# ScalarE's load of the table for Gelu and its copy of the last turned rows of the MLP change places

## What is computed

```python
attn_out = attn_out @ out_w + out_b + residual
out = rmsnorm(attn_out, postnorm_w)
out = jax.nn.gelu(out @ mlp_w1 + mlp_b1) @ mlp_w2 + mlp_b2
return out + residual
```

## Time and profile before

| what | value |
|---|---|
| median of 3 runs | 1889.08 us (1888.2 to 1889.91) |
| the profiled execution | 1890.01 us, of which the span is 1888.0 us |
| TensorE busy | 1640.7 us, 87% |
| VectorE busy | 1215.1 us, 64% |
| ScalarE busy | 894.8 us, 47% |
| GpSimd busy | 780.4 us, 41% |
| mean granted clock of TensorE | 0.94 |

### The profile page before, as it was taken

One profiled execution on the slowest core, in us unless ns is written; L12 is line 12 of the kernel. 1 busy time (PEld: TensorE's weight loads), 2 busy tenths in 40 slices (PEclk: granted clock), 3 DMA queues, 4 the chain that ended last, 5 costly groups with the idle time before them and its releaser, 6 DMA issues.

```text
span 1888.0 us, 34749 instructions
## 1 busy us (share of the span) xinstructions
PE 1640.7 (87%) x13615; PEld 1023.1 (54%) x13615; DVE 1215.1 (64%) x2153; ACT 894.8 (47%) x1855; POOL 780.4 (41%) x871
## 2 busy tenths in 40 slices
PE   5898998899997898888988989889998889889735
PEld 3675555565564655655555655646456465555303
DVE  4742478655886468855687457864588646983483
ACT  4454554545544445545454456444555544554202
POOL 5631249404573147702485034840457214770000
PEclk9998898999999999999988999999999999999857
DMA  6001014200331005100141101410042100510060
GB/s 186 1 2 36 1 21 55 42 23 1 44 43 35 19 1 69 25 28 19 18 55 22 44 4 24 62 36 19 1 53 36 33 19 1 69 25 1 13 91 11
DMA packets 73567, 60.78 MB, mean 32 GB/s; under 512 B 38960, under 2 KB 56512, under 8 KB 73408
## 3 DMA queue, kind: packets, MB, share of 16 engines
q1 hardware_dynamic: 55648, 47.99, 17.4%
q10 hardware_dynamic: 17216, 10.55, 2.0%
q0 software_dynamic: 544, 0.03, 0.0%
HBM read 20.28 MB, written 4.19 MB: 13 GB/s over the span
## 4 chain that ended last, share of the span: by engine, by line
PE 66%; DVE 14%; ACT 8%; POOL 6%; issue 4%; DMA 0%; DVEq 0%; SPq 0%; ACTq 0%; POOLq 0%
PE bank L638 26%; PE bank L777 8%; PE bank L1019 6%; DVE late L1316 6%; PE bank L957 5%; PE bank L654 4%; PE bank L982 3%; PE bank L717 2%; POOL soft_ring L1685 2%; PE bank L910 2%; POOL late L1640 2%; ACT soft_ring L1149 2%; PE bank L975 1%; PE bank L886 1%; DVE late L1328 1%
## 5 line engine op out<-in xcount | busy, mean ns | idle before, releaser
L1685 POOL TENSOR_TENSOR soft_ring<-soft_ring,seg_max 128x512 f32<-128x512 f32 x256 | 282.0, 1117 | 304.5 <-DVE seg_max L1482 303.8
L1164 ACT ACTIVATE soft_ring<-soft_ring 128x512 f32<-128x512 f32 x256 | 159.9, 625 | 177.6 <-POOL soft_ring L1685 177.6
L1316 DVE TENSOR_TENSOR_SCAN late<-late 128x520 f32<-128x520 f32 x128 | 220.7, 1724 | 12.6 <-POOL late L1642 9.4
L777 PE MATMUL bank<-early 32*128 32x128 f32 (+2 forms) x1024 | 152.5, 416 | 38.8 <-ACT soft_ring L1149 36.0
L957 PE MATMUL bank<-ident,soft_ring 128*128 128x128 f32 x1024 | 166.2, 292 | 22.6 <-ACT soft_ring L1164 19.8
L1640 POOL TENSOR_TENSOR late<-late 128x520 f32<-128x520 f32 x112 | 174.6, 1559 | 15.7 <-DVE late L1316 15.4
L957 PEld LDWEIGHTS bank<-ident,soft_ring 128*128 128x128 f32 x1024 | 116.3, 146 | 102.8 <-issue 53.4
L1482 DVE TENSOR_REDUCE seg_max<-soft_ring 128x8 f32<-128x512 f32 (+1 forms) x256 | 166.6, 675 | 0.2
L1693 POOL TENSOR_SCALAR soft_ring<-soft_ring,rden 128x256 f32<-128x256 f32 x64 | 65.5, 1023 | 215.4 <-DVE rden L1444 215.4
L1047 ACT ACTIVATE late<-bank 128x512 f32<-128x512 f32 (+2 forms) x104 | 60.5, 595 | 158.6 <-PE bank L638 158.4
L638 PE MATMUL bank<-early,w 128*128 128x512 f32 x256 | 120.6, 622 | 15.9 <-ACT early L1221 15.9
(11 more groups left out here) (257 smaller groups left out, 3310.1 us busy)
## 6 DMA issues: line engine op xcount, KB each, us to landing
late<-late SPq DMA_DIRECT2D x128, 260.0 KB, 4.5
c<-in_ctx ACTq DMA_DIRECT2D x8, 512.0 KB, 4.1
x<-in_x ACTq DMA_DIRECT2D x8, 512.0 KB, 4.9
out_x<-late SPq DMA_DIRECT2D x8, 512.0 KB, 2.9
mask<-in_mask_Bx1xSxS_ff ACTq DMA_DIRECT2D x16, 128.0 KB, 3.9
mask<-in_mask_BxS_ik SPq DMA_DIRECT2D x8, 256.0 KB, 3.3
w<-in_L_xattn_mlp_w SPq DMA_DIRECT2D x2, 1024.0 KB, 9.6
wkv<-in_L_xattn_kv_w SPq DMA_DIRECT2D x1, 512.0 KB, 3.8
```

The lines of the kernel that those rows point to most:

```text
L777: ins = mm(t[:, width * n:width * n + width], lhsT, rhs, start=True, stop=True)
L1164: af(soft[:, u % SOFT, :], soft[:, u % SOFT, :], ACT.Exp).then_inc(sig("exp"), 1)
L1316: nc.vector.tensor_tensor_scan(sj[:, n % 2, :], wP[:, k, :, :].rearrange("p b t -> p (b t)"), aj[:, n % 2, :], 0.0, ALU.mult, ALU.add).the ...
L1685: tt(s, s, seg_max[:, u % SOFT, 0:segs].unsqueeze(2).broadcast_to([128, segs, 512 // segs]), ALU.subtract).then_inc(sig("sub"), 1)
```

## The change

Inside ScalarE's loop, where the h = 1 half is copied, `tables(GELU)` now stands ahead of the wait for the bank and of the two copies. The later call of `tables(GELU)`, behind the loop, stays in the text but issues nothing, since that set is held already. There are as many table loads as before (55 in ScalarE's list); the compiler adds none. No other engine's list changes.

```diff
                         if i == A2 + 8 * h + 17:
+                            if h == 1:
+                                tables(GELU)
                             t, free = take(act, ("xnT", h))
                             for k in range(KT):
                                 ins = af(xnT[:, h, k, :], t[:, 256 * k:256 * k + 256], ACT.Identity, scale=v("post", k))
```

## The result

The changed kernel took 1911.36 us in the median of 4 runs (1907.55 to 1919.5), against 1888.64 (1887.97 to 1889.91) for the kernel before. The ratio is 1.0113, with a 95% interval of 1.0076 to 1.015. It is slower, as forecast, by 22.7 us rather than 18.4, inside the range. Both kernels scatter more than the first runs showed: 29 later runs of the kernel before, on one chip, went from 1883 to 1908 with a median of 1893.9, and six of the changed kernel beside them had 1913.83, a ratio of 1.0112 (1.0076 to 1.0147). The medians lie 19.9 apart, but the interval is too wide to decide between the two.

A forecast was written before the change was run, and what follows sets the result against it. The prediction took TensorE, waiting for ScalarE's late copies in seven groups, as the bound. 9.9 us for the load plus 8.5 for the clock, 18.4 on 1889.08, gave 1907.5 us, range 1898 to 1915.

The forecast's parts named there:

- The bound and the path: Late groups: the end of ScalarE's copies sets u 0, then "project", the moments and layer 3's tail; first group costs 0.
- The first term: Copies in the seven late groups: the load delays them and u 0 by 1.42 each, 9.9 us in all.
- The waits on the copies: TensorE's idle time ahead of u 0: forecast to come to about 25.8 us, not 15.9.
- The rival with a drain behind each load: Late groups' copies: the load brings a further wait, moving them by 2.77; 1917 us, chance 0.03.
- The first Gelu drain: Second group, on ScalarE: forecast to start 3.3 after the copies instead of 4.6.
- The second term: u 0 and u 1: TensorE's clock falls in all seven late groups, five more than before, 5 x 1.69 = 8.5 us.
- the longer low level: Rival, behind late groups' idle time: low clock holds longer, each loses 2.7; 1914.5 us, chance 0.09.
- One or two falls more or fewer elsewhere: Clock falls elsewhere in the program: taken as the forecast's own range, 1902 to 1913 us.
- The rival "the clock does not follow": Late groups: the load costs 9.9 and the clock's falls stay at two; 1899.0 us, chance 0.14.

The follow-up runs named there:

- first-group: Changed against the kernel before: load ahead of the copies in the first group alone; 1891.99 us against 1893.15, ratio 0.9995.
- late-group runs: Changed against the kernel before: load ahead of the copies in the second to eighth group only; 1914.19 us, ratio 1.0108.
- after: The changed kernel, load ahead of the h = 1 copies in all groups, against the kernel before; 1911.36 us, ratio 1.0113.
- second load: The changed kernel with one more table load, of another set, ahead of the moved one; 1920.69 us, ratio 1.0121 to the kernel before.
- copy on VectorE: The kernel before with the h = 1 copies done by VectorE, ahead of the gate, in all groups; 1884.74 us against 1890.65, ratio 0.9961.
- three plain delays: The kernel before with one, two or three linked scratch copies ahead of the late groups' copies, no load moved; 1897.52, 1897.55 and 1911.5 us.
- second group alone: Changed against the kernel before: load ahead of the copies in the second group only; 1893.18 us against 1890.65, ratio 0.9999.
- The run with TensorE kept busy: The changed kernel with three matmuls on static weights ahead of u 0 in the late groups; 1909.8 us, ratio 1.0085 to the kernel before.

## Why the prediction was right, and where it was off

**The bound and the path: right.** TensorE waited for late copies in seven groups and in the first for nothing more than before. The first-group and late-group runs put the loss in the seven.

**The first term: right.** I forecast 1.42 per late group; the idle time grew by 1.43. Seven times that is 10.0, and squares to u 0 grew by 10.2 to 10.8. The waits on the copies were to come to 25.8 and did. The rival with a drain behind each load, at 0.03, is refuted by the 1.31 in after and by the 1.29 of the second load. The page behind it (the Trainium skill, "ScalarE: Activation LUTs", section "What ACT_TABLE_LOAD costs") adds about 1380 ns of drain to 1283 ns of load; the traces agree with the second number, and the measurement decides against the first. The first Gelu drain came 3.3 after the copies, as forecast and for the forecast reason: the last transfer was issued at 379.45 and the drain started at 379.50. The view names L638 for the 2.48 ahead of it, but the last matmul of u 0 had ended at 379.05.

**The second term: the step that was off.** I took a fall of the clock in all seven late groups, since 22 of 22 idle stretches of 2.7 us or more had been followed by one. The recorded executions of after had it in five of seven, twice, and the late-groups-only kernel in four. The MLPs lost 6.1, 7.1 and 4.4 rather than the forecast 8.5. Over all kernels a fall followed 4 of 20 idle times of 2.1 at this place, 1 of 7 of 2.57, 2 of 7 of 3.03, 20 of 29 of 3.5 and all 7 of 4.82. The count of 22 is right, but it was of other places: behind 21 of them TensorE resumed with matmuls of 64x256, 128x128 or 128x256, and behind one alone with 128x512, as u 0 does. I counted stretches by their length alone; whether the kind of work makes the difference, no run here tests. So the term was too large: it measured about 6 against 8.5. The MLPs of after's second, third and fourth late group show its kinds (length; PE, PEld, DVE, ACT, POOL; clock; DMA; GB/s):

```profile
602.40:637.24 34.84, 34.08 (x113) 21.39 (x114) 14.57 (x46) 15.88 (x24) 0.00 (x0) 0.95 0.13 38
827.67:860.81 33.14, 32.38 (x113) 20.80 (x114) 14.56 (x45) 15.88 (x24) 0.00 (x0) 1.00 0.13 40
...
1055.78:1091.61 35.83, 35.07 (x113) 21.83 (x114) 14.57 (x45) 15.88 (x24) 0.00 (x0) 0.92 0.13 38
```

The first has the 1.70 of one fall, the second none, and the third the longer low level, 2.69, that I had as a rival for all seven. It came once in this execution and twice in the repeated one.

**A third term was missing.** "One or two falls more or fewer elsewhere", taken as noise around nought, were 6.1 us in the attention of each recorded execution of after, and 6.5 in late groups only. The clock is lower there (0.93 for 0.96 in the third group). That is more than the second term was too large by: 10 + 6 + 6 is 22 us, against 9.9 + 8.5. Two errors of opposite sign, 2.4 too much and 6 left out, kept the sum within a fifth of the measured 22.7, and that is partly luck. The term is not the delay's alone: the attention also grew by 5.9 where u 0 came earlier (copy on VectorE), by only 2.6 to 2.8 under the three plain delays, and by 0.2 with the second group alone. Its cause stays open.

**The rival "the clock does not follow"** gave 9.9. The run with TensorE kept busy goes further, with no fall at u 0 at all, and still lost 16.7 us, so the rival was wrong in its own way: taking the falls at u 0 away left the load's 10 and 9.7 in the attention.

## What to carry to other kernels

A load of tables belongs where its engine waits anyway. Look for the row with the long idle time behind it (here 5.37 ahead of "moments 2"), and not for the first place at which it is legal; ahead of a copy for which TensorE waits it costs its full length in every round but the one where the copy itself had to wait. If the copy is what TensorE waits for, move the copy to an engine that is idle there: that gained 0.4% (0.15% to 0.64%) where the reordering lost 1.1%.

## What was not expected of the hardware

The falls of the granted clock make the time of this kernel a sum whose terms are not independent: about 0.9 us of delay in each of seven groups cost 0.25%, 1.4 us cost 1.0 to 1.1%, and taking out every fall at one place returned a fifth to a quarter of that, with intervals that overlap. The same kernel's runs on one chip spread over 1883 to 1908 us, so for changes of a few us at TensorE's idle times one needs tens of runs, and a single trace's ledger is good for the local terms only.
